# A three-block transformer kernel on one core: gate and up weight tiles prepared in turns beside the first FFN steps, and preparation blocks of 512 columns

## The reference

```python
x = x + 0.5 * ffn(layernorm(x), w_gate, w_up, w_down)
x = x + attn(layernorm(x), w_qkv, w_out, q_gain)
x = x + 0.5 * ffn(layernorm(x), w_gate, w_up, w_down)
# ffn:  (silu(x @ w_gate.T) * (x @ w_up.T)) @ w_down.T     512 -> 2048 -> 512
# attn: 16 heads of 32, unit-normed q and k, rope on even heads, gain per head, causal softmax
```

## Time and profile before

| | |
|---|---|
| runs | 2797.44 us median (2796.15 to 2797.51) |
| profiled execution | 2798.85 us, span 2797.1 us |
| mean granted TensorE clock | 0.994 |
| PE busy | 2726.2 us, 97% |
| DVE busy | 1780.7 us, 64% |
| ACT busy | 1205.0 us, 43% |
| POOL busy | 531.2 us, 19% |
| DMA moved | 39.37 MB, mean 14 GB/s |

### The profile page before, as it was taken

One profiled execution on the slowest core, in us unless ns is written; L12 is line 12 of the kernel. 1 busy time (PEld: TensorE's weight loads), 2 busy tenths in 40 slices (PEclk: granted clock), 3 DMA queues, 4 the chain that ended last, 5 costly groups with the idle time before them and its releaser, 6 DMA issues.

```text
span 2797.1 us, 56089 instructions
## 1 busy us (share of the span) xinstructions
PE 2726.2 (97%) x22720; PEld 1992.9 (71%) x22720; DVE 1780.7 (64%) x5054; ACT 1205.0 (43%) x2250; POOL 531.2 (19%) x820
## 2 busy tenths in 40 slices
PE   4999999999999999999999999999999999999999
PEld 4677766777767777777767777677777776777776
DVE  7766666666656565666656666565666767676643
ACT  5443544354434434443434445344443444454422
POOL 0012132213130302213121121312203131313100
PEclk8999999999999999999999999999999999999999
DMA  7000000000000000000000000000000000000000
GB/s 257 1 16 1 16 1 1 1 17 16 2 1 16 16 2 1 1 16 16 2 1 9 9 16 1 1 16 9 8 5 13 16 2 1 1 16 9 2 9 16
DMA packets 16577, 39.37 MB, mean 14 GB/s; under 512 B 1472, under 2 KB 1472, under 8 KB 15808
## 3 DMA queue, kind: packets, MB, share of 16 engines
q1 hardware_dynamic: 16320, 35.79, 3.6%
HBM read 26.35 MB, written 9.44 MB: 13 GB/s over the span
## 4 chain that ended last, share of the span: by engine, by line
PE 87%; DVE 8%; issue 3%; ACT 2%; DMA 0%; POOL 0%; SPq 0%; DVEq 0%; ACTq 0%
PE psum L1045 25%; PE psum L1046 25%; PE psum L1047 25%; PE psum L1200 2%; PE psum L1176 2%; PE psum L1212 2%; PE psum L1068 1%; PE psum L1154 1%; PE psum L1158 1%; DVE arena L885 1%; DVE arena L883 1%; DVE arena L960 1%; PE psum L1213 1%; DVE arena L889 1%; ACT arena L775 1%
## 5 line engine op out<-in xcount | busy, mean ns | idle before, releaser
L1045 PE MATMUL psum<-arena,WG 128*128 128x256 f16 x2048 | 558.8, 273 | 4.9 <-DVE arena L885 3.4
L1045 PE MATMUL psum<-arena,WU 128*128 128x256 f16 x2048 | 558.9, 273 | 0.0
L1047 PE MATMUL psum<-arena,WG 128*128 128x256 f16 x2048 | 558.7, 273 | 0.0
L1047 PE MATMUL psum<-arena,WU 128*128 128x256 f16 x2048 | 558.5, 273 | 0.0
L1046 PE MATMUL psum<-arena,WU 128*128 128x256 f16 x2048 | 558.5, 273 | 0.0
L1046 PE MATMUL psum<-arena,WG 128*128 128x256 f16 x2048 | 558.5, 273 | 0.0
L883 DVE SCALAR_TENSOR_TENSOR arena<-arena,psum 128x256 f32<-128x256 f32 x512 | 214.8, 420 | 446.2 <-ACT arena L775 445.2
L775 ACT ACTIVATE arena<-psum,tscale 128x256 f32<-128x256 f32 x512 | 241.1, 471 | 564.4 <-PE psum L1047 563.7
L1045 PE MATMUL psum<-WD,arena 128*128 128x512 f16 x1024 | 388.8, 380 | 3.6 <-DVE arena L889 3.5
L1047 PE MATMUL psum<-WD,arena 128*128 128x512 f16 x1024 | 388.4, 379 | 0.0
L1046 PE MATMUL psum<-WD,arena 128*128 128x512 f16 x1024 | 388.4, 379 | 0.0
(11 more groups left out here) (145 smaller groups left out, 4465.2 us busy)
## 6 DMA issues: line engine op xcount, KB each, us to landing
arena<-in_L_attn_x SPq DMA_DIRECT2D x16, 512.0 KB, 3.7
out<-arena SPq DMA_DIRECT2D x16, 512.0 KB, 2.8
arena<-in_L_ffn_w_gate SPq DMA_DIRECT2D x4, 1024.0 KB, 9.2
arena<-in_L_ffn_w_up SPq DMA_DIRECT2D x4, 1024.0 KB, 7.3
WD<-in_L_ffn_w_down SPq DMA_DIRECT2D x4, 1024.0 KB, 12.5
arena<-in_L_attn_w_qkv SPq DMA_DIRECT2D x1, 3072.0 KB, 22.2
arena<-in_L_attn_w_out SPq DMA_DIRECT2D x1, 1024.0 KB, 6.7
park<-arena SPq DMA_DIRECT2D x2, 512.0 KB, 2.8
```

Of the source, the lines that this page charges most:

```text
L1045: T_.matmul(o, lhs(0), rhs(0), start=first, stop=False)
L1047: return T_.matmul(o, lhs(1), rhs(0), start=False, stop=last)
```

## The change

- Gate and up tiles alternate (gate rows 0 to 511, up rows 0 to 511, gate rows 512 to 1023, ...). A gate tile and an up tile serve four steps. Tiles 0 and 1 and the first two token tiles are made ahead of step 0. The other six are made in pairs beside pieces 0 to 24, eight pieces to a pair; gates and ups 0, 4, 8 and 12 wait for their tile's low parts.
- A tile's turn is cut in four (one bank each, of five banks in rotation); `w rows` is cut in two, and for tile 0 `w scales` and the load too. One of the four small operations is folded away.
- The raw tiles lie in w_down's final memory instead of the arena, raw w_down in the arena, and the first two normalized token tiles in w_qkv's memory.
- SyncE issues tile 0 ahead of the rope table and the gains; w_qkv and w_out are loaded after the last w_down turn instead of right behind w_down. The gains are prepared at piece 48 instead of first.
- w_down's turns come three at a time before pieces 24 to 29, its scales before piece 31, its parts before pieces 32 to 46.
- All of DVE's `wd max`, `magnitude` and `weights` blocks have 512 columns (16 of each), and those that need no wait behind them have none. ACT's `weights` blocks are cut in the same way. Magnitudes stand before pieces 40 to 55, scales 56, weights 58 to 73, pickers 76 to 82. Token tiles 2 and 3 are normalized from piece 34 on instead of 24; those of batches 2 and 1 two steps later than before.

```diff
-        put(("w scales", 0), ("w rows", 0), ("w scales", 1))
-        for j in range(8):
...
-            put(("w turn", j))
-            if j == 7:
-                put(("stats", 0, 0, 0), ("stats", 0, 0, 1), ("norm", 0, 0, 0), ("turn", 0, 0, 0), ("norm", 0, 0, 1))
-            put(("w out", j))
...
-        late = {n + 1: [("wd turn", n), ("wd out", n)] + [("wd max", n // 4)] * (n % 4 == 3) for n in range(HC)}
-        late[19] = [("wd scales", 0)]
+        put(("w scales", 0), ("w rows", 0, 0), ("w rows", 0, 1), *turns(0, 0, 1, 2, 3), ("w scales", 1))
+        put(("stats", 0, 0, 0), *parts_of(0, 0, 1), ("stats", 0, 0, 1), ("w rows", 1, 0), ("w rows", 1, 1), *parts_of(0, 2, 3))
+        put(("norm", 0, 0, 0), ("norm", 0, 0, 1), *turns(1, 0, 1), ("turn", 0, 0, 0), ("split", 0, 0, 0), *turns(1, 2, 3))
+        put(*parts_of(1, 0, 1), ("turn", 0, 0, 1), ("split", 0, 0, 1), *parts_of(1, 2, 3), ("w scales", 2))
+        late = {n: [] for n in range(100)}
+        for i in range(3):
+            a, b, n = 2 * i + 2, 2 * i + 3, 8 * i
+            m = n + (i == 0)
+            late[n] += [("w rows", a, 0)]
+            late[n + 1] += [("w rows", a, 1), ("w scales", b)]
+            late[m + 2] += turns(a, 0, 1)
+            late[m + 3] += turns(a, 2, 3) + parts_of(a, 0, 1)
+            late[m + 4] += parts_of(a, 2, 3)
+            late[n + 4] += [("w rows", b, 0)]
+            late[n + 5] += [("w rows", b, 1)] + [("w scales", a + 2)] * (i < 2)
+            late[n + 6] += turns(b, 0, 1)
+            late[n + 7] += turns(b, 2, 3) + parts_of(b, 0, 1)
+            late[n + 8] += parts_of(b, 2, 3)
+        for m in range(HC):
+            late[24 + m // 3] += [("wd turn", m), ("wd out", m)]
+            late[25 + m // 3] += [("wd max", m // 4, i) for i in range(4) if m % 4 == 3]
+        late[31] += [("wd scales", 0)]
         for k in range(HC):
-            late[20 + k] = [("wd parts", k)]
...
+            late[32 + k - (k > 0)] += [("wd parts", k)]
+        normalize(WHEN, 0, 0, (2, 3))
+        late[48] += [("gains",)]
+        for n in range(HC):
+            late[40 + n] += [("magnitude", n)]
+        late[56] += [("scales", 0, 0)]
+        for n in range(HC):
+            late[58 + n] += [("weights", n)]
...
+            def w_turn(j, k):
+                if k == 0:
+                    pe.wait_ge(s["wscaled"], 2 * (j + 1))
+                if 4 * j + k >= 5:
+                    pe.wait_ge(s["w_lo"], 4 * j + k - 4)
...
+                if j < HC and j % 4 == 0:
+                    pe.wait_ge(s["w_lo"], 2 * j + 4)
...
+            sp.wait_ge(s["dn_tr"], HC)
             sp.dma_start(RAWQ, w_qkv.rearrange("(k p) n -> p k n", p=P)).then_inc(s["qkv_in"], 16)
...
+            def magnitude(m):
...
+                block = RAWQ[:, m // 3, m % 3 * D:(m % 3 + 1) * D] if m < 3 * KC else RAWO[:, (m - 3 * KC) * D:(m - 3 * KC + 1) * D]
+                counted(V_.tensor_reduce(qmax[:, m:m + 1], block, AX_X, ALU.max, apply_absolute_value=True))
```

More of the change, by code:

```diff
@@ L83, in build @@
     xn = [words("xn"), words("qt", 0, D)]
+    xn += [WQ.rearrange("p s k n -> p (s k n)").bitcast(F32)[:, i * D:(i + 1) * D] for i in range(2)]
     XT = [halves(n).rearrange("p (s k n) -> p s k n", s=2, k=KC) for n in ("xt", "xt2")]
@@ L172, in ps16, with w_bank, projection_block, w_columns @@
         return psum[:, b * 512:(b + 1) * 512].bitcast(F16)
-    def wd_bank(m):
-        return (0, 1, 2, 6, 7)[m % 5]
+    TURN_BANKS = (0, 1, 2, 6, 7)
+    def w_bank(j, k):
+        return TURN_BANKS[(4 * j + k) % 5]
+    def projection_block(n):
+        if n < KC:
+            return WO[:, :, n], RAWO[:, n * D:(n + 1) * D], 2
+        k, c = (n - KC) // 3, (n - KC) % 3 * D
+        return WQ[:, :, k, c:c + D], RAWQ[:, k, c:c + D], 1
+    def wd_bank(m):
+        return TURN_BANKS[(32 + m) % 5]
+    def w_columns(j):
+        return (WU if j % 2 else WG), slice(512 * (j // 2), 512 * (j // 2 + 1))
+    def w_stats(j, first=0, n=4):
+        at_ = HC * (j % 2) + 4 * (j // 2) + first
+        return slice(at_, at_ + n)
     QSEG = {3: 0, 2: 512, 0: 896, 1: 1024}
@@ L447, in order, with turns, parts_of @@
-        late.update({52 + 4 * k: [("weights", 0, k)] for k in range(KC)})
+        def turns(j, *chunks):
+            return [("w turn", j, k) for k in chunks]
+        def parts_of(j, *chunks):
+            return [("w out", j, k) for k in chunks]
+        put(("w scales", 0), ("w rows", 0, 0), ("w rows", 0, 1), *turns(0, 0, 1, 2, 3), ("w scales", 1))
+        put(("stats", 0, 0, 0), *parts_of(0, 0, 1), ("stats", 0, 0, 1), ("w rows", 1, 0), ("w rows", 1, 1), *parts_of(0, 2, 3))
+        put(("norm", 0, 0, 0), ("norm", 0, 0, 1), *turns(1, 0, 1), ("turn", 0, 0, 0), ("split", 0, 0, 0), *turns(1, 2, 3))
@@ L448, in order @@
+        for n in range(HC):
+            late[58 + n] += [("weights", n)]
+        for g in range(GH):
+            late[76 + 2 * g] += [("pickers", g)]
+        put(*late[0])
         while ("split", 0, 1, 1) not in seen or at[0] < first_piece[2, 0, HC] - 12:
@@ L484, in xn_of @@
     def xn_of(b, u, t):
+        if (b, u) == (0, 0) and t < 2:
+            return 2 + t
         return t % 2 if (b, u) in ((0, 0), (B - 1, 2)) else 0
@@ L670, in _, with scale_rows, w_out @@
         def _(act):
[L671 to L675, removed]
-                ins.then_inc(s["wscaled"], 1)
[L678 to L682, removed]
+            def scale_rows(j, half):
+                act.wait_ge(s["wsent"], j + 2 if j else 1 + half)
+                for i in (2 * half, 2 * half + 1):
+                    r = RAW[j % 4][:, i, :]
+                    ins = nc.scalar.activation(r, r, ACT.Copy, scale=wscale[:, w_stats(j, i, 1)])
+                ins.then_inc(s["wscaled"], 1)
+            def w_out(j, k):
+                W, c = w_columns(j)
+                act.wait_ge(s["w_tr"], 4 * j + k + 1)
+                nc.scalar.activation(W[:, 0, k, c], ps(w_bank(j, k)), ACT.Copy).then_inc(s["w_hi"], 1)
             def wait(name, k):
@@ L821, in w_scales @@
[L821 to L837 removed]
+            def w_scales(j):
+                for i in range(0, 4, 2 if j == 0 else 4):
+                    if j:
+                        c, rows = w_stats(j), RAW[j % 4]
+                        dve.wait_ge(s[f"raw{j % 4}"], 16 * (j // 4 + 1))
+                    else:
+                        c, rows = w_stats(0, i, 2), RAW[0][:, i:i + 2, :]
+                        dve.wait_ge(s["half0" if i else "raw0"], 16)
+                    link(V_.tensor_reduce(wmax[:, c], rows, AX_X, ALU.max, apply_absolute_value=True))
+                    link(V_.tensor_scalar(wpow[:, c], wmax[:, c], LEAST, 2.0 ** -13, ALU.max, ALU.mult))
+                    link(V_.tensor_scalar(wpow[:, c].bitcast(I32), wpow[:, c].bitcast(I32), EXP_BITS, None, ALU.bitwise_and))
+                    V_.reciprocal(wscale[:, c], wpow[:, c]).then_inc(s["wsent"], 1)
+                if j % 2 == 0:
+                    link(V_.tensor_scalar(tscale[:, w_stats(j)], wpow[:, w_stats(j)], 2.0 ** -10, None, ALU.mult))
+                if j == 7:
+                    link(V_.scalar_tensor_tensor(out=pgu[:, :], in0=wpow[:, 0:HC], scalar=2.0 ** 31, in1=wpow[:, HC:2 * HC], op0=ALU.mult, op1=ALU.mult))
@@ L1026, in scales, with weights @@
                 dve.wait_ge(s["scales"], 2)
-            def weights(out_, k):
-                dve.wait_ge(s["pro_hi"], 1 if out_ else k + 2)
-                W, raw, c = ((WO, RAWO, 2) if out_ else (WQ[:, :, k:k + 1], RAWQ[:, k], 1))
-                V_.scalar_tensor_tensor(out=W[:, 1].rearrange("p k n -> p (k n)"), in0=raw, scalar=gscale[:, c:c + 1],
-                                        in1=W[:, 0].rearrange("p k n -> p (k n)"), op0=ALU.mult, op1=ALU.subtract).then_inc(s["pro_lo"], 1)
-            run({"w scales": w_scales, "w out": w_out, "wd max": wd_max, "wd scales": wd_scales, "wd parts": wd_parts, "magnitude": magnitude, "scales": scales, "weights": weights,
+            def weights(n):
+                dve.wait_ge(s["pro_hi"], n + 1)
+                W, raw, c = projection_block(n)
+                V_.scalar_tensor_tensor(out=W[:, 1], in0=raw, scalar=gscale[:, c:c + 1], in1=W[:, 0], op0=ALU.mult, op1=ALU.subtract).then_inc(s["pro_lo"], 1)
+            run({"gains": gains, "w scales": w_scales, "w out": w_out, "wd max": wd_max, "wd scales": wd_scales, "wd parts": wd_parts, "magnitude": magnitude, "scales": scales, "weights": weights,
                  "stats": stats, "norm": norm, "split": split, "gated": gated, "parts": parts, "residual": residual,
```

130 lines of the change are left out of this document (67 added, 63 removed).

## The result

| | before | changed |
|---|---|---|
| median of the runs | 2797.51 us (2796.15 to 2798.93, 5 runs) | 2783.20 us (2782.52 to 2784.34, 5 runs) |
| span of the profiled execution | 2797.1 us | 2780.5 us |
| mean granted clock | 0.994 | 0.998 |

The changed kernel takes 0.9948 of the time of the one before, 95% interval 0.9934 to 0.9963: 14.3 us less by the medians, 16.6 us less by the two spans. Forecast were 2779 us, in a range of 2769 to 2790.

The account below looks back on a forecast made before the run. PE bound most of the span, but some 44 us of it were empty at the start. 20 us gained at step 16, 0 behind, less 1.75 for a slow spell: 18.5 us, forecast 2779 us, range 2769 to 2790.

Parts of the forecast that it names:

- its own signs of being wrong: Pair over 20 us, clock under 0.9 from 30 to 75 us, or span behind step 16 differing by over 4 us.
- Until the first gate product: Start of the kernel to gate 0: 60 us becomes 22 us, with ends of 21 and 28 us.
- Six tiles beside steps 0 to 11: Pairs of tiles beside four steps each, DVE the bound: 18, 17 and 17 us; piece 24 at 75 us with slips.
- w_down's turns: Pieces 24 to 31: first down product 21.6 us after piece 24, 4 us later than PE could.
- Downs 0 to 13: Stretch up to step 16: DVE 21 us against PE's 18.1; step 16 at 118 us against 138.20, 20 us gained.
- Blocks of 512 columns: Pieces 46 to 73, behind step 16: old 2.4 us wait and 1.75 us clock loss removed, crowding added; net zero.
- the scales 2.8: Pieces 46 to 73: the scales counted as 2.8 us within 41 us of DVE work.
- The terms put at nothing: Gains' preparation at piece 48, raw tiles' places, token buffers, qkv's transfer: no cost; other end for qkv 4 us of DVE.
- the first (turns serialize): Tile pairs beside the steps do not overlap as queues allow, 20 to 21 us each: costs 10.5 us, 2789; chance 0.18.
- the fourth (clock stays low): Clock stays at 1.2 GHz through the mixed stretch because PE works in bursts: 49 us more, 2828; chance 0.03.
- The third: No gain: start slips to 28 us, pairs take 21 us, qkv waits; about 2798 to 2800; chance 0.03.
- The term for one slow spell: After the 4 us wait before the first w_down product: one new spell at 1.2 GHz, 1.75 us lost.

Follow-up runs that it names:

- Experiment 3: Changed kernel with tiles 2 to 7 prepared before piece 0, so no gate or up tiles beside steps 0 to 11: 2808.54 us, ratio to before 1.0041.
- experiment 4: Changed kernel with w_down's turns five, four, four, three before pieces 24 to 27, reductions, scales and parts one piece earlier: 2781.17 us, ratio to before 0.9942.
- experiment 8: Changed kernel with the moves of experiment 1 and experiment 4, and token tiles 2 and 3 normalized from piece 20 instead of 34: 2769.88 us, ratio to before 0.9902.
- experiment 1: Changed kernel with scales of w_qkv and w_out before piece 62 instead of 56, their parts before pieces 63 to 78: 2774.21 us, ratio to before 0.9917.
- experiment 2: Kernel before with scales of w_qkv and w_out before piece 56 instead of 47, parts and pickers later too: 2804.93 us, ratio 1.0028.
- experiment 5: Changed kernel with the diffs of experiment 1 and experiment 4 together: 2771.37 us, ratio to before 0.9907.
- experiment 6: Experiment 1 with the old large blocks for parts of w_out and w_qkv, one of 2048 and four of 1536 columns: 2779.85 us, ratio to before 0.9936.

## Why the prediction was right, and where it was off

The sum was 18.5 us of span and came out as 16.6. That it came out so near is in part luck, as two errors of opposite sign partly cancel. With its slow spell in it, the prediction gave 18.5 us at gate 16 and nothing behind it; measured were 21.3 us and a loss of 4.7. Behind gate 16 its own signs of being wrong came true: the span there differs by 4.7 us from before (its bound was 4), and a single wait was 7.6 us where all were to be under 1. By its own steps:

- **Until the first gate product.** 22 us forecast, 22.12 measured. The places on the way came near too: the first sixteen transposes ended at 13.7 us (13 forecast), those of the two token tiles at 18.5 and 20.6 (17.6 and 20.5).
- **Six tiles beside steps 0 to 11.** Pairs at 18, 17 and 17 us; measured 18.28, 15.20 and 17.38 between the gates, the last with 1.3 us of w_down's turns in it. Piece 24's own work began at 71.7, not 75. DVE was near its bound (35.5 of 39.6 us busy, where over 90% was forecast). The second pair is under the lower end of 16.1; that PE carried some of DVE's lag across the pairs' borders would explain it and is not shown. The slow clock was put at the start; it came at 29.8, after a wait of 2.4 us. Experiment 3 shows the overlap itself: some 20 of 25.6 us at gate 12.
- **w_down's turns.** The first down product 21.6 us after piece 24, forecast; 93.36 - 71.67 = 21.7 measured, its wait 4 against 4.06, and the slow spell behind it as summed. Why it is late was right only in part: 4.4 us of DVE idle between 70 and 80 us were in it (experiment 4).
- **Downs 0 to 13.** Gate 16 at 118 us, or 43.1 after piece 24; measured 116.89, or 45.2. The stretch took 2.1 us more than forecast, and DVE stood 3.8 us in it for POOL's power behind the swap. The prediction took a token tile as 2.35 us of DVE and did not ask when POOL could make its power. How much of the 2.1 us is this wait stays open; experiment 8, which took it away together with other work, gained 1.4 us at gate 16.
- **Blocks of 512 columns.** Here a step failed: the zero was wrong twice. "I set this at zero: what the blocks give, crowding takes." In experiment 1, with the swap out of the way, crowding took nothing: 74.33 us from gate 16 to gate 32 against 78.51 before, the 4.2 us of the old wait and its slow clock in full. The loss in the changed kernel is the scales' exchange, priced as part of "the scales 2.8": it took 7.6 us of PE and 1.5 of clock. The trace before showed the exchange only with 43 or 20 us of POOL idle ahead of it, where the swap costs nothing.
- **The terms put at nothing.** w_qkv's transfer landed 10.2 us after its issue, and nothing waited for it. The gains' preparation and the buffers cost nothing either: gate 32 to the end is the same within 0.1 us.

Of the rivals, the first (turns serialize) and the fourth (clock stays low) are refuted by the pairs' times and the clock of 1.00. The third was added up wrongly: a loss of 22 us on top of the forecast of 2779 is 2801 us, not 2798 to 2800. The term for one slow spell was right for the wait named; in all there were three.

Open: how the 10.7 us of the swap back divide (it was 10.7 to 11.3 in the runs here, and at most 10.1 before, where the power was asked for by then), how much of the gain of experiment 8 is the swap's, and how much of the remaining 22 us at the start could still go.

## What to carry to other kernels

Work that fills an engine's wait at the start is worth the difference between what it frees and what it crowds: here 38 us freed gave 21 at gate 16, and each stretch up to there could be summed from rows to within 3.5 us. When stages move, list for each engine what now stands directly in front of what, GpSimd with its few short operations too: a pair of operations that was always 20 us apart can hide a cost that no row has. And where one engine holds an in-order queue for another's answer, put other work between question and answer.

## What the runs showed of the hardware that was not expected

- From the end of POOL's power to the start of its exchange across partitions 5.84 to 6.03 us pass when the exchange is asked for at once (four runs, of both kernels' orders: the changed kernel and experiments 2, 3 and 4). When it is asked for 6.6 us after the power's end (experiment 1), nothing of it is seen. The way back took 10.7 to 11.3 us in the changed kernel and experiments 1, 3, 4, 5 and 6, and at most 10.1 in the kernel before.
- In the changed kernel the granted clock was 1.00 at the first gate product (22.1 us), right behind a start with PE 40% busy, and fell only after a wait of 2.4 us. Before, where PE had been busy 2.4 of the last 10 us, the first gate product began at 1.2 GHz (0.50). A wait of 1.85 us in experiment 4 had the clock at 1.00 behind it.
- The row of the start prints 1.00 throughout, but its first sixteen transposes took 0.23 us each (3.65/16) and the first token tile's four 1.12 us, against 0.13 each (1.04/8) and 0.63 to 0.66 for four later on. So this 1.00 doesn't say at what pace PE ran before about 19 us; the transposes do.
- Mixed transposes and products, with short waits and banks in rotation, ran at 1.00 for 39.6 us with PE 95% busy (33.4 to 73.0 us). The clock of the fourth rival, that stays low or goes back and forth in such work, did not occur in them.
